# New orders for all five queues in the image stage, and VectorE's weighted product moved to fourth place in the expert step

## What is computed

```
h = patches_layernormed @ W + b + pos              # 196 rows of 192 for each image
h = concat([h, txt], axis=1)                       # 324 rows for each image
h = h + ssm(layernorm(h))                          # state scan over 324 rows, 16 states, 192 channels
h = h + moe(layernorm(h))                          # shared expert + top 6 of 128 routed experts
# ssm:    state = exp(delta*A)*state + delta*B*x ;  y = sum over the 16 states of state*C
# routed: silu(x @ Wg) * (x @ Wu) @ Wd, times the routing weight, added to each token's row (192 slots an expert)
# shared: silu(x @ Wsg) * (x @ Wsu) @ Wsd, 928 wide
```

## Time and profile before

| what | value |
|---|---|
| median of three runs | 4759.75 us (4747.87 to 4792.27) |
| profiled execution, its own time | 4760.37 us |
| its span, first to last instruction | 4758.6 us |
| busy share of the span: PE, DVE, ACT, POOL | 83%, 72%, 55%, 63% |
| mean granted TensorE clock | 0.939 of full speed |
| HBM traffic over the span | 99 GB/s |

### The profile page before, as it was taken

How to read it: one execution, slowest core, us unless ns; L and a number is a source line. 1 busy time by engine, 2 the same in 40 slices (tenths; PEclk the granted TensorE clock), 3 DMA queues, 4 the chain that set the end, 5 groups by cost and what they waited for, 6 DMA issues and landing times. The chain is left out here.

```text
span 4758.6 us, 74520 instructions
## 1 busy us (share of the span) xinstructions
PE 3971.8 (83%) x22114; PEld 2963.9 (62%) x22114; DVE 3441.9 (72%) x5523; ACT 2596.9 (55%) x4807; POOL 2997.6 (63%) x1609
## 2 busy tenths in 40 slices
PE   4458888888888888888888888887887899899987
PEld 3345556655555565655566565555556788788877
DVE  1888888888787888878788888888516565566554
ACT  1467766766677666767766677766632222222221
POOL 0877777767676777767777777777404555555555
PEclk8579999999999999999999999999998999999999
DMA  3322323322232233222323332322107777777775
GB/s 84 78 74 69 91 70 82 89 79 75 70 88 72 70 84 87 78 75 70 91 70 84 93 77 70 91 60 74 41 14 182 177 177 177 173 184 181 180 171 127
DMA packets 243533, 473.54 MB, mean 100 GB/s; under 512 B 39644, under 2 KB 162080, under 8 KB 243220
## 3 DMA queue, kind: packets, MB, share of 16 engines
q1 hardware_dynamic: 203792, 429.90, 34.0%
q0 software_dynamic: 36864, 37.98, 5.3%
q10 hardware_dynamic: 2564, 1.82, 0.2%
HBM read 404.99 MB, written 64.56 MB: 99 GB/s over the span
## 5 line engine op out<-in xcount | busy, mean ns | idle before, releaser
L506 POOL TENSOR_TENSOR y<-y,state 128x972 f32<-128x972 f32 x448 | 1017.1, 2270 | 731.9 <-DVE state L667 730.7
L661 DVE TENSOR_TENSOR_SCAN ps<-ps,state 128x972 f32<-128x972 f32 x512 | 1115.2, 2183 | 131.8 <-ACT ps L529 100.6
L485 POOL TENSOR_TENSOR state<-du,b_rows 128x972 f32<-128x972 f32 x512 | 1164.1, 2290 | 10.4 <-POOL delta L496 7.1
L529 ACT ACTIVATE ps<-delta,a_neg 128x324 f32<-128x324 f32 x1536 | 732.9, 524 | 311.3 <-DVE state L667 281.0
L1039 POOL DMA_INDIRECT out_rows<-yo,scatter_idx x256 | 369.5, 1443 | 458.7 <-DMA out_rows<-yo,scatter_idx 266.9
L667 DVE TENSOR_TENSOR state<-ps,c_rows 128x972 f32<-128x972 f32 x512 | 591.0, 1164 | 22.2 <-DVE ps L661 0.5
L781 PE MATMUL ps<-ws_d,inter 116*98 116x192 f32 (+1 forms) x3072 | 549.0, 333 | 63.3 <-DVE inter L753 24.6
L781 PEld LDWEIGHTS ps<-ws_d,inter 116*98 116x98 f32 (+1 forms) x3072 | 503.4, 176 | 93.4 <-issue 32.7
L753 DVE TENSOR_TENSOR inter<-ag,ps 116x648 f32<-116x648 f32 x256 | 211.5, 826 | 447.3 <-PE ps L766 447.3
L763 PE MATMUL ps<-x2f,ws_g 128*116 128x324 f32 x1024 | 366.4, 484 | 170.7 <-DVE inter L753 165.9
L1170 PE MATMUL e_ps<-w_down,e_inter 116*96 116x192 f32 x2048 | 394.7, 351 | 98.9 <-DVE yo L1120 98.6
(11 more groups left out here) (172 smaller groups left out, 7554.5 us busy)
## 6 DMA issues: line engine op xcount, KB each, us to landing
c_rows<-bc_rows SPq DMA_DIRECT2D x256, 324.0 KB, 4.8
...
w_lo<-in_we_up SPq DMA_DIRECT2D x128, 348.0 KB
w_down<-in_we_down SPq DMA_DIRECT2D x128, 348.0 KB
...
w_lo<-in_we_up SPq DMA_DIRECT2D x128, 116.0 KB
```

What stands on the lines that cost most here:

```text
L485: nc.gpsimd.tensor_tensor(b.state[n % 4][:], b.du[t.p][:], row, ALU.mult).then_inc(input_ready, 1)
L506: nc.gpsimd.tensor_tensor(y, y, b.state[n % 4][:], ALU.add).then_inc(y_added, 1)
L529: ins = nc.scalar.activation(to[:, c * L:c * L + L], b.delta[t.p][:, c, :], ACT.Exp, scale=b.a_neg[:, c, k:k + 1])
L661: nc.vector.tensor_tensor_scan(s, s, b.state[k % 4][:].rearrange("p a t -> p (a t)"), 0.0, ALU.mult, ALU.add).then_inc(scan_done, 1)
```

## The change

Nothing is added to or taken from what is computed. The five lists of the image stage are replaced by other orders of nearly the same pieces: ACT's `decay` of state 0 and POOL's `fill_b` of state 0 stand at the head of a body in place of the end of the body before; one of PE's eight `warm` pieces, `(2, 0)`, goes, and one, `(1, 0)`, comes at the end of the body. In body -1 alone the embedding pieces are put last. In the expert step DVE's `down` moves from the first to the fourth place. The change is announced with "two down buffers" as well; in the code, `w_down` has four buffers and `yo` two before and after, and `down_ps` is one PSUM tile before and after: no line of the diff touches a buffer. Line numbers of the changed kernel are higher by 1 below line 114.

```diff
     "pe": (
-        ("up_u", 2, 4), ("warm", 2, 4), ("x1_turn", -1, 2), ("bc_values", -1, 0), ("up_g", 2, 5), ("gate", 1, 0), ("gate", 1, 1), ("up_u", 2, 5),
-        ("warm", 2, 5), ("step", -1, 0), ("step", -1, 1), ("up_g", 2, 6), ("warm", 2, 6), ("step", -1, 2), ("up_u", 2, 6), ("up_g", 2, 7), ("warm", 2, 7),
-        ("up_u", 2, 7)
...
     "dve": (
-        ("scan", 0, 5), ("ln2_stats", 1, 0), ("up_u", 2, 0), ("emb_scale", -1, 0), ("find", 2, 0), ("fill_c", 0, 5), ("scan", 0, 6), ("ln2_apply", 1, 0),
+        ("ln2_stats", 1, 0), ("scan", 0, 5), ("find_a", 2, 0), ("ln2_apply", 1, 0), ("emb_scale", -1, 0), ("fill_c", 0, 5), ("up_u", 2, 1),
...
-    return [x for x in SCHEDULE[engine] if (PAIRS - 1 if x[0] in ("find_a", "find") else 0) <= i - x[1] < PAIRS]
+    todo = [x for x in SCHEDULE[engine] if (PAIRS - 1 if x[0] in ("find_a", "find") else 0) <= i - x[1] < PAIRS]
+    return sorted(todo, key=lambda x: x[1] == -2 and x[0][:3] == "emb") if i == FIRST_BODY + 1 else todo
...
-    "dve": (("down", 2), ("up", 0, 0), ("up", 0, 1), ("weigh", 0), ("token", -5), ("one_hot", -6), ("dot", -1)),
+    "dve": (("up", 0, 0), ("up", 0, 1), ("weigh", 0), ("down", 2), ("token", -5), ("one_hot", -6), ("dot", -1)),
```

More of the change, by code:

```diff
@@ L62 @@
     "pe": (
[L63 to L66, removed]
@@ new lines @@
+        ("warm", 2, 1), ("up_g", 2, 2), ("x2_turn", 1, 0), ("find", 2, 0), ("emb_a", -2, 1), ("up_u", 2, 2), ("warm", 2, 2), ("emb", -2, 1),
+        ("x2_turn", 1, 1), ("up_g", 2, 3), ("x2_turn", 1, 2), ("up_u", 2, 3), ("warm", 2, 3), ("x1_turn", -1, 0), ("up_g", 2, 4), ("x1_turn", -1, 1),
+        ("x1_turn", -1, 2), ("up_u", 2, 4), ("bc_values", -1, 0), ("up_g", 2, 5), ("gate", 1, 0), ("warm", 2, 4), ("gate", 1, 1), ("step", -1, 0),
+        ("up_u", 2, 5), ("step", -1, 1), ("up_g", 2, 6), ("warm", 2, 5), ("step", -1, 2), ("up_u", 2, 6), ("warm", 2, 6), ("up_g", 2, 7), ("warm", 2, 7),
@@ L70 @@
+        ("up_u", 2, 7), ("warm", 1, 0)
     ),
     "act": (
-        ("down", 3, 0), ("decay", 0, 1), ("decay", 0, 2), ("resid", 1, 0), ("down", 3, 1), ("decay", 0, 3), ("decay", 0, 4), ("resid", 1, 1), ("down", 3, 2),
-        ("up_g", 2, 0), ("to_exp", 2, 0), ("resid", 1, 2), ("decay", 0, 5), ("count", 2, 0), ("emb_a", -2, 0), ("count", 2, 1), ("ln2_stats", 1, 0),
-        ("decay", 0, 6), ("up_g", 2, 1), ("emb_a", -2, 1), ("to_exp", 2, 1), ("ln2_apply", 1, 0), ("decay", 0, 7), ("ln1_stats", -1, 0), ("emb", -2, 0),
@@ L79 @@
-        ("softplus", -1, 0), ("decay", 0, 15), ("up_g", 2, 7), ("to_exp", 2, 7), ("decay", -1, 0)
+        ("decay", 0, 0), ("decay", 0, 1), ("down", 3, 0), ("decay", 0, 2), ("emb_a", -2, 0), ("resid", 1, 0), ("down", 3, 1), ("decay", 0, 3),
+        ("emb_stats", -1, 0), ("decay", 0, 4), ("resid", 1, 1), ("down", 3, 2), ("up_g", 2, 0), ("decay", 0, 5), ("resid", 1, 2), ("decay", 0, 6),
+        ("to_exp", 2, 0), ("count", 2, 0), ("ln2_stats", 1, 0), ("up_g", 2, 1), ("count", 2, 1), ("to_exp", 2, 1), ("emb_a", -2, 1), ("emb", -2, 0),
@@ new lines @@
+        ("ln2_apply", 1, 0), ("decay", 0, 7), ("ln1_stats", -1, 0), ("up_g", 2, 2), ("to_exp", 2, 2), ("x2_turn", 1, 0), ("ln1_apply", -1, 0),
+        ("decay", 0, 8), ("decay", 0, 9), ("x2_turn", 1, 1), ("up_g", 2, 3), ("x2_turn", 1, 2), ("emb", -2, 1), ("to_exp", 2, 3), ("decay", 0, 10),
+        ("x1_turn", -1, 0), ("up_g", 2, 4), ("x1_turn", -1, 1), ("to_exp", 2, 4), ("x1_turn", -1, 2), ("decay", 0, 11), ("decay", 0, 12),
+        ("bc_values", -1, 0), ("up_g", 2, 5), ("gate", 1, 0), ("decay", 0, 13), ("gate", 1, 1), ("to_exp", 2, 5), ("step", -1, 0), ("decay", 0, 14),
@@ L80 @@
+        ("decay", 0, 15), ("step", -1, 1), ("up_g", 2, 6), ("to_exp", 2, 6), ("step", -1, 2), ("softplus", -1, 0), ("up_g", 2, 7), ("to_exp", 2, 7)
     ),
     "dve": (
-        ("choose", 2, 0), ("choose", 2, 1), ("choose", 2, 2), ("scan", 0, 0), ("scan", 0, 1), ("fill_c", 0, 0), ("fill_c", 0, 1), ("scan", 0, 2),
-        ("weigh", 2, 0), ("fill_c", 0, 2), ("scan", 0, 3), ("fill_c", 0, 3), ("scan", 0, 4), ("weigh", 2, 1), ("find_a", 2, 0), ("fill_c", 0, 4),
-        ("scan", 0, 5), ("ln2_stats", 1, 0), ("up_u", 2, 0), ("emb_scale", -1, 0), ("find", 2, 0), ("fill_c", 0, 5), ("scan", 0, 6), ("ln2_apply", 1, 0),
@@ L85 @@
[L85 to L88 removed]
+        ("choose", 2, 0), ("choose", 2, 1), ("choose", 2, 2), ("scan", 0, 0), ("fill_c", 0, 0), ("scan", 0, 1), ("fill_c", 0, 1), ("scan", 0, 2),
@@ L93 @@
[L93 to L95 removed]
+        ("fill_c", 0, 0), ("fill_b", 0, 0), ("fill_b", 0, 1), ("fill_b", 0, 2), ("fill_b", 0, 3), ("fill_c", 0, 1), ("fill_b", 0, 4), ("fill_c", 0, 2),
```

30 lines of the change are left out of this document (14 added, 16 removed).

## The result

The changed kernel takes 4340.9 us (median of three runs, 4339.7 to 4342.7) against 4759.8 us: a ratio of 0.911, 95% interval 0.904 to 0.918.

A forecast was written before the change was run, and what follows sets the result against it. Bounds: in the image stage the order of four partly idle engines, in the expert stage the scatter chain. Profiled 4760.4 us - 252 (image) + 13 (expert) = 4521 us, range 4400 to 4645 us.

The forecast's parts named there:

- The DVE part: Image body from `choose` to the third product G*U, bound by DVE: 57.7 us becomes 50.4, net 7.3 us less.
- the image sum: Image bodies 3 to 30: 10.0 us a body saved, 1 us taken off, so 9.0 us a body, 252 us.
- The five intervals: Image body from third to eighth product G*U, each waiting for PE: 43.8 us becomes 41.1, 2.7 us less.
- interval (4): Fourth of the intervals between products: 9.6 to 7.2 us, as a `step` and its exchange with ACT leave it.
- interval (3): Third of the intervals between products: 13.0 to 13.3 us, with `gate` split by a `warm` and a `step` before U.
- The first bodies: Image bodies ahead of body 3, embedding last in body -1: left at 0, with the last within 15 us either way.
- The expert step: Expert stage, `yo` moved behind both products: 0.1 us a step more, 13 us in all, bounds -38 to +115.
- ACT's extra table load: Image body, at the decays: one table load more, 1.28 us, costed at 0, bounds 0 to 36 us over 28 bodies.
- more gain: Rival, image stage: PE the only bound left, 372 us less there, 4401 us in all; chance 0.12.
- The expert loop pays in full: Rival, expert stage: +115 us there, image stage as forecast, 4623 us in all; chance 0.13.
- no gain: Rival, image body: the second part lengthens as much as the DVE part shortens, 4731 us in all; chance 0.08.
- slower: Rival, image body: waits with POOL move to some eleven small operations, body 12.0 us longer, 5109 us; chance 0.06.

The follow-up runs named there:

- the second of its runs: The kernel before, with `ln1_apply` alone moved ahead of `fill_c` 6 on VectorE: 4630.3 us, ratio 0.971 to before.

## Why the prediction was wrong, and where it was right

**The DVE part** came out near the forecast: 7.9 us less in the mean body where 7.3 were counted, but partly by luck. `ln1_apply` was put at 6.1 us; the exchange by itself is worth 3.4 to 3.5 us in this part. In the second of its runs DVE's busy time there falls by 5.6 us, near the 6.1, and 2.0 us of it come back as waits. What the other edits gave, some 4.4 us together, is more than the 1.2 that were counted for them (2.2 + 2.0 - 3.0); they were not tried singly. In the body shown the first product waits for nothing and the second 0.27 us, where 2.2 us were counted for the two. The rule of the Trainium skill ("SBUF — State Buffer", "Who interferes with whom"), that the one that starts first holds the port for its whole instruction, agrees with the 2.12 and 2.16 us of the run with ln1_apply put back beside POOL's 2.24. The rival built on it, that the loss moves to other operations, did not come true: none of L650 to L652 and L711, the eleven small operations of a body, exceeds 168 ns from 605 to 2900 us.

**The step that failed in the image sum** is the second part of the body: "Sum: 43.8 to 41.1, 2.7 us less", and behind it "I take 1 us off: 9.0 us", because PE and ACT would have almost no slack. The five intervals lose 4.7 us, not 2.7, and nothing is lost to late hand-overs; with 0.6 us more from the DVE part that is 2.0 + 1.0 + 0.6 = 3.6 us a body, and 28 x 3.6 = 102 us of the error. Of the 2.0 us, 0.8 come from one body taken for all (43.8 us, the mean is 44.6; its interval (4) was 9.6 us, the mean is 10.4), and most of the rest from interval (3), which was to grow by 0.3 us and fell by 0.8.

What the runs showed in place of the missing slack: PE's "89.6 us of work a body" were no fixed floor. Durations of matmuls were taken from the trace of before as if they belonged to the instructions. The earlier trace rows showed that they don't: the G product behind the gap took 2.19 us and a later one 1.35. The prediction counted that difference in one interval and not in the rest. With the gaps closed, PE's work is 85.4 us a body, 4.2 less (by the granted clocks of 0.964 and 0.995 a body has 7.5 us at the lower level before and 0.9 us after, an estimate), and PE's idle time falls all the same, from 14.8 to 5.9 us. That closing a gap by itself shortens the body is shown (useless work in the gap: 1.5 us a body), and so is that opening one lengthens it (the run with four warm pieces fewer). How the 4.7 us divide between waits and clock is not shown by a run. The granted clock of the five intervals before answers to 5.7 us at the lower level, so that the clock can have given back 2.9 us at most, an estimate; in intervals (2) and (5) it was 1.00 before, and there only waits and places of pieces changed. Of the 354 us of the 28 bodies, the exchange of `ln1_apply` accounts for 124 to 128; the other moves are read from the traces and were not tried one by one.

**The first bodies** were left at 0, because their order had its own line in the change. That line does nothing; the table does, and gains 28.4 us up to the choose of body 3. With the last bodies (5.4 us) that is another 34 us.

**The expert step** failed at "The scatter chain stays at 9.0 us", and with it at "that chain is the bound, not PE". The two lengths were right (9.0 and 8.2 us), and the chain that ended last before does run through landings; but 8.2 us was PE's busy time alone, and with the 98.9 / 128 = 0.8 us that it waited for `yo` PE's loop had 9.0 us as well. It was `yo` that tied the two loops together: standing first in DVE's step it held both products and PE's `down` until a landing, and the stop cost PE its clock. The price that the prediction did put on the new place, 0.8 to 1.0 us a step for PE at `yo`, is what is measured (102.1 / 128 = 0.8); overlooked was that the old place cost the same 0.8 us on average, in fewer and longer stops, and 34.8 us of slower matmuls on top. The line of the page that shows it, `yo` waiting 325.8 us for the scatter, stands in none of the rows. That is 31.7 + 13 = 45 us of the error. The lower bound of -38 us holds the measured -31.7, by luck: its reason, loads that collide less with a scatter, was not tried. Together 102 + 34 + 45 = 181 us, the distance between the forecast of 4521 us and the measured 4340.9 but for rounding.

**Costs put at nothing.** ACT's extra table load is there, with its 1283 ns; that it costs nothing is not shown, since no run takes it out alone. The Trainium skill ("ScalarE: Activation LUTs", "What ACT_TABLE_LOAD costs") adds a drain of about 1.38 us to each switch, by which one more switch a body would be an estimated 75 us with its load. The trace does not agree as to the drain: it shows 0.9 us of idle time ahead of all 50 loads at the decays together. SP's loads were not tried by themselves.

**Of the rivals**, "more gain" (PE the only bound, 13.3 us a body) is nearest in the image stage, with 12.6, though not for its reason: PE's work was not a fixed floor, and PE still idles 5.9 us a body. "The expert loop pays in full", "no gain" and "slower" are refuted.
